# Two transformer layers with gated cross-attention: ScalarE places the negated maxima and stores the bounds

## The chip, the cores and the metric

The kernel runs on one core of a Trainium2 chip. The core has a matrix engine (TensorE, PE), a vector engine (VectorE, DVE), a scalar engine (ScalarE, ACT), GpSimd (POOL), a sync engine (SP) whose instructions start transfers, and 16 DMA engines. Each engine works through its own list of instructions in order, and they wait for each other by semaphores. The metric is the device time of one execution in microseconds.

## What is computed

The input is `x` (8 batches x 256 rows x 256) and a context (8 x 256 x 192). Four steps follow each other, each added to `x` behind a normalisation and with a gate: cross-attention, a mixture of experts, cross-attention again (with scores clipped to +-10000), and a second mixture of experts. The two attentions matter here:

```python
q = (x @ q_w + q_b).reshape(B, N, H, hd).transpose(0, 2, 1, 3)      # 16 heads of 16
attn = jnp.einsum('bhnd,bhmd->bhnm', q * scale, k)
attn = jnp.clip(attn, -CLAMP, CLAMP)                                # layer 1 only
attn = jax.nn.softmax(attn, axis=-1)
out = jnp.einsum('bhnm,bhmd->bhnd', attn, v)
```

A softmax over the keys needs the largest score of each query first, so that the exponential does not overflow.

## The kernel before

**Units and pairs.** A unit is one batch of one attention: units 0 to 7 are layer 0, units 8 to 15 layer 1. In a unit the 16 heads are taken as 8 pairs: heads 0 to 7 are side 0, heads 8 to 15 side 1, and pair p is head p of either side. A function `base(u)` gives the time slot in which unit u begins; a unit takes 8 slots, one pair in each. Layer 0's experts (`gate_up`, `down0`: L849, L859) fill the slots from about 105 us to 530 us, so TensorE has products to do beside both attentions. The second experts run alone at the end.

**The scores are computed twice.** `scores_by_query(u, p)` (L752) makes a pair's scores with queries on the partitions; VectorE takes the row maxima (`maxima`, L1368). Ten slots later `scores_by_key(u, p)` (L773) makes them again with keys on the partitions, which is the form that the product with the values needs, and ScalarE takes the exponential (`exponentials`, L1162). There the maximum must be subtracted along the free dimension, and TensorE does it: queries and keys are stacked in tiles `stack_q` and `stack_k`, side 0 on partitions 0 to 63 and side 1 on 64 to 127. Of each side 48 rows are the high and low parts of the 16 features; rows 48 and 49 of `stack_q` hold the negated maximum of each query in two parts, and the same rows of `stack_k` hold ones.

**How the maxima get there.** When a unit's 8 pairs are through (slot `base(u)` + 7), `shifts(u)` on VectorE (L1379 to L1382) writes three rows of 32 numbers per query tile: the high part, the low part, and for layer 1 the lower bound -max - 10000. In slot `base(u)` + 8 TensorE turns them (`shift_turn`, L759) and ScalarE copies them to `shiftT` (L1151; in layer 1 L1150 writes the exponential of the bounds first). Then the sync queue's `place_shift(u)` waits for `shiftT_ready` and issues four transfers (L566), one for each side and part, each into one partition of `stack_q`, and in layer 1 a fifth, L569, which stores the bounds to DRAM. `scores_by_key(u, 0)`, two slots later, waits for the four (`shift_in`). In layer 1 the sync queue's `load_lower` (L577) waits for the stored bounds (`lower_out`) and loads a pair's, spread over all partitions; VectorE's `clip` (L1393) uses them.

**What stands around it in the queues.** The order of every engine's work is written out by `make_plan`: an entry at `2g` or `2g + 1` belongs to slot g. `shift_turn` of unit u is put in front of `qprod` of unit u+2, at the same entry. So ScalarE's list has, in slot `base(u)` + 8: the exponential of a pair of the unit before, `shift_turn(u)`, and `qprod(u + 2)`, which copies the high part of the queries (L1074). VectorE subtracts it to get the low part (L1359), and both are stored to DRAM by the sync queue (`store_queries`, L529 and L532), which stands behind `place_shift(u)` in that queue. Units 14 and 15 have no `qprod` there. Three PSUM banks serve all products but the scores and the values in turn; a product may take its bank only when the one three uses before has been read, and the bank of `qprod` counts as read when L1359 is done. ScalarE issues few transfers of its own: five small ones at the start, and the queries of unit 0 (L1079, L1082), each behind a wait for the instruction that wrote them.

Of the kernel before, what the change touches and what calls it, by code (L numbers as in the profile page):

```python
# [12 lines left out]
F32 = mybir.dt.float32  # L13
F32R = mybir.dt.float32r
# [3 lines left out]
ALU = mybir.AluOpType  # L18
# [7 lines left out]
H, HD = 16, 16  # L26
TT = S // P
# [15 lines left out]
CLAMP = 10000.0  # L43
# [5 lines left out]
FULL = PARTS * HD  # L49
HALF = 64  # L50
PAIRS = H // 2
# [5 lines left out]
SETS = 3  # L57
# [36 lines left out]
def layer_of(u):  # L94
    return u // NB


def batch_of(u):
    return u % NB


def base(u):

    return LEAD + PAIRS * u
# [143 lines left out]
def build(nc, a, out):  # L248
    es = ExitStack()
    first = ExitStack()  # L250
    sem = Semaphores(*[es.enter_context(nc.semaphore(name)) for name in SEMAPHORES])
# [5 lines left out]
    def sba(name, shape, dt=F32):  # L257
        return first.enter_context(nc.sbuf_tensor(name, shape, dt))

    qk_dram = [nc.dram_tensor(f"qk_{l}", (NB, 4, D, S), F32).ap() for l in range(2)]  # L260
    lower_dram = nc.dram_tensor("lower", (NB, H * TT, P), F32).ap()
# [38 lines left out]
    stack_q = [sba(f"stack_q{i}", [P, PAIRS, S], F32R) for i in range(SETS)]  # L300
# [18 lines left out]
    rowmax = [sba(f"rowmax{i}", [P, 2, PAIRS, TT]) for i in range(2)]  # L319
    shift = sba("shift", [P, 3, H * TT])  # L320
    shiftT = sba("shiftT", [3 * H * TT, P])
# [113 lines left out]
    def _(sp):  # L435
# [121 lines left out]
                    o = HALF * side + blk * HD  # L557
                    sp.dma_start(stack_q[i][o:o + HD, :, :].bitcast(F32), src[side]).then_inc(q_in[i], 16)

        def place_shift(u):  # L560
            l, b = layer_of(u), batch_of(u)
            sp.wait_ge(sem.shiftT_ready, u + 1)
            for side in range(2):
                for part in range(2):
                    row, src = HALF * side + FULL + part, (2 * part + side) * PAIRS * TT
                    sp.dma_start(stack_q[u % SETS][row:row + 1, :, :].bitcast(F32).rearrange("o a (t q) -> o (a t) q", t=TT),  # L566
                                 shiftT[src:src + PAIRS * TT, :]).then_inc(sem.shift_in, 16)
            if l:
                sp.dma_start(lower_dram[b], shiftT[2 * H * TT:3 * H * TT, :]).then_inc(sem.lower_out, 16)  # L569

        def load_lower(u, p):
            b = batch_of(u)
            j = PAIRS * b + p
            if j >= 3:
                sp.wait_ge(sem.clip_done, j - 2)
            sp.wait_ge(sem.lower_out, 16 * (b + 1))
            sp.dma_start(lower[j % 3][:, :, :], lower_dram[b].rearrange("(h a t) q -> a h (t q)", h=2, t=TT)[p]  # L577
                         .partition_broadcast(P)).then_inc(lower_in[j % 3], 16)

        def store_alternative(_):  # L580
            sp.wait_ge(sem.zalt_ready, 1)
            sp.dma_start(zalt_dram[:, :], zalt).then_inc(sem.zalt_out, 16)

        def load_alternative(_):
            sp.wait_ge(sem.zalt_out, 16)
            sp.wait_ge(sem.y_done, N0 * NB)
            sp.dma_start(alt_rows.rearrange("p b d -> p (b d)"),
                         zalt_dram.rearrange("b d -> (b d)").partition_broadcast(P)).then_inc(sem.zalt_in, 16)
# [30 lines left out]
        def first_weights(_):  # L619
            sp.wait_ge(sem.counted, NB)  # L620
            sp.dma_start(b1[:, :], a["L1_ffn_b1"]).then_inc(sem.biases_in, 16)
            sp.wait_ge(sem.block_ready, 1)
            for i in range(2):
                load_w1(i)

        def store_rows(b):
# [5 lines left out]
        load_x(0)  # L632
        load_ctx(0)
        stages = {"load": load, "ctx": context, "kprod": store_keys, "qprod": store_queries, "stack_keys": stack_keys, "stack_queries": stack_queries,
                  "shift_turn": place_shift, "mean_project": store_alternative, "project": store_z, "reload": reload, "load_expert": load_expert, "load_alternative": load_alternative,
                  "weights1": store_rows, "bias1": store_x, "tables": first_weights}
        for g in range(SLOTS_IN_ALL):
            for stage, n in PLAN[2 * g - 3] + PLAN[2 * g - 2]:
# [2 lines left out]
            u, p = divmod(g + 1 - base(0) - LAG, PAIRS)  # L641
# [12 lines left out]
    def _(pe):  # L654
# [6 lines left out]
        def stay_busy(n, bank):  # L661

            for _ in range(n):
                pe.matmul(bank[:, 0:P], ident[:, :], ident[:, :], start=True, stop=True)
# [97 lines left out]
        def scores_by_key(u, p):  # L762
            i, sq, sk = PAIRS * u + p, stack_q[u % SETS], stack_k[u % SETS]
            if p == 0:
                pe.wait_ge(sem.shift_in, 64 * (u + 1))
            if i:
                pe.wait_ge(sem.exp_done, i)
            if i < PAIRS:
                stay_busy(2, by_key[:, 0, :])
            for kt in range(2):  # L770
                for side in range(2):
                    rows = slice(HALF * side, HALF * side + HALF)
                    mm = pe.matmul(by_key[:, side, kt * S:kt * S + S], sk[rows, p, kt * P:kt * P + P], sq[rows, p, :],  # L773
                                   start=True, stop=True)
            mm.then_inc(sem.qk2_done, 1)
# [46 lines left out]
        def gate_turn(_):  # L822
            bank = open_bank("gate_turn", 0)
            pe.wait_ge(sem.gates_in, 64)
            for k in range(KC):
                tr = pe.transpose(bank[:, k * E0:k * E0 + E0], gate_rows[:, k * P:k * P + P], ident[0:E0, 0:E0])
            tr.then_inc(sem.gate_turned, 1)
# [35 lines left out]
        def spread_nan(_):  # L863
            bank = open_bank("spread_nan", 0)
            pe.wait_ge(sem.flag_ready, 1)
            pe.matmul(bank[:, 0:1], ones[:, :], flag[:, 1:2], start=True, stop=True).then_inc(sem.flag_mm, 1)

        def mean_v(_):
            bank = open_bank("mean_v", 0)
            pe.wait_ge(sem.ctxT_ready, NB)  # L870
            for k in range(2):
                mm = pe.matmul(bank[0:NB, 0:D], ctx_sum[:, k, :], wkv[1][0:CROWS, k, D:2 * D], start=k == 0, stop=k == 1)
            mm.then_inc(sem.mean_mm, 1)
# [67 lines left out]
        for g in range(SLOTS_IN_ALL):  # L941
            v, q = divmod(g - base(0), PAIRS)
            if 0 <= v < UNITS:
                scores_by_query(v, q)
            u, p = divmod(g - base(0) - LAG, PAIRS)
# [7 lines left out]
            u, p = divmod(g - base(0) - LAG - 3, PAIRS)  # L953
# [90 lines left out]
    def _(ac):  # L1044
# [96 lines left out]

        def shift_turn(u):
            if u:
                ac.wait_ge(sem.shift_in, 64 * u)
            if u > NB:
                ac.wait_ge(sem.lower_out, 16 * (u - NB))
            bank, bounds = banks[BANK_OF["shift_turn", u][0]], slice(2 * H * TT, 3 * H * TT)
            ac.wait_ge(sem.shift_turned, u + 1)
            if layer_of(u):
                ac.activation(shiftT[bounds, :], bank[bounds, 0:P], ACT.Exp)  # L1150
            ac.activation(shiftT[0:2 * H * TT, :], bank[0:2 * H * TT, 0:P], ACT.Copy).then_inc(sem.shiftT_ready, 1)  # L1151

        def gates(_):
            ac.wait_ge(sem.gates_in, 32)
            ac.activation(tg[:, :], g_raw[:, :], ACT.Tanh).then_inc(sem.gates_ready, 1)
# [60 lines left out]
        for g in range(SLOTS_IN_ALL):  # L1216
# [3 lines left out]
            u, p = divmod(g - base(0) - LAG, PAIRS)  # L1220
# [81 lines left out]
    def _(dv):  # L1302
# [66 lines left out]
                             AX, ALU.max).then_inc(sem.max_done, 1)  # L1369

        def shifts(u):
            flat = rowmax[u % 2][:, :, :, :].rearrange("p h a t -> p (h a t)")
            dv.wait_ge(sem.max_done, PAIRS * (u + 1))
            if layer_of(u):
                dv.tensor_scalar(flat, flat, CLAMP, -CLAMP, ALU.min, ALU.max).then_inc(sem.shift_chain, 1)
                dv.wait_ge(sem.shift_chain, u + 1 + batch_of(u))
            if u:
                dv.wait_ge(sem.shift_turned, u)
            dv.tensor_scalar(shift[:, 0, :].bitcast(F32R), flat, -1.0, None, ALU.mult).then_inc(sem.shift_chain, 1)  # L1379
            dv.tensor_scalar(shift[:, 2, :], flat, -1.0, -CLAMP, ALU.mult, ALU.add).then_inc(sem.shift_ready, 1)  # L1380
            dv.wait_ge(sem.shift_chain, u + 1 + (batch_of(u) + 1 if layer_of(u) else 0))
            dv.scalar_tensor_tensor(shift[:, 1, :].bitcast(F32R), flat, -1.0, shift[:, 0, :], ALU.mult,  # L1382
                                    ALU.subtract).then_inc(sem.shift_ready, 1)

        def clip(u, p):
# [374 lines left out]
        for g in range(SLOTS_IN_ALL):  # L1760
# [7 lines left out]
            v, q = divmod(g - base(0), PAIRS)  # L1768
# [7 lines left out]
            u, p = divmod(g - base(0) - LAG - 1, PAIRS)  # L1776
# [216 lines left out]
```

## Time and profile before

| what | value |
|---|---|
| median of 3 runs | 982.74 us (978.57 to 985.58) |
| the profiled execution | 982.38 us |
| its span | 980.6 us |
| granted clock of TensorE, mean | 0.951 |
| busy: TensorE, VectorE, ScalarE, GpSimd | 92%, 75%, 48%, 26% |
| sync queue, wait for ScalarE's copy L1151 | 68.3 us in 14 waits |
| placing transfers L566 | 64 of 8 KB, issue median 0.589 us |

The span is the time from the first to the last instruction of the profiled execution. A granted clock of 1.00 is full speed, 0.50 the lower level. An engine's busy share is an average over stages with different limits, so the rows below are taken from single stretches. SPq and ACTq are the parts of the sync engine and of ScalarE that issue transfers; issuing is not counted as busy.

### The profile page before, as it was taken

How to read it: one execution, taken by the hardware profiler on the slowest of the kernel's cores; microseconds unless marked ns; L12 is line 12 of the kernel's file. 1: busy time of each engine (PE TensorE's matmuls, PEld its weight loads, DVE VectorE, ACT ScalarE, POOL GpSimd, SP SyncE). 2: the span in 40 equal slices, each digit the busy share in tenths (PEclk: the TensorE clock that was granted, in tenths of full speed). 3: DMA queues.
4: the chain of work that ended last, by engine and by line, in shares of the span. 5: the costliest groups of instructions: out<-in, count | busy, mean ns of one | idle time of the engine just before them, and what ended most of it. 6: DMA issues, size and time to landing. Idle time of an engine off the chain costs nothing.

```text
span 980.6 us, 18579 instructions
## 1 busy us (share of the span) xinstructions
PE 905.1 (92%) x6641; PEld 746.2 (76%) x6641; DVE 740.2 (75%) x1516; ACT 471.6 (48%) x835; POOL 252.5 (26%) x385
## 2 busy tenths in 40 slices
PE   7998999999999998999988877899899999999995
PEld 6766677777767766777756554667799999999995
DVE  4555767677676767798887898978868788887783
ACT  2245544444534343344433444443356666666773
POOL 7511011020210000010101113323136566543331
PEclk9999999999999999999999977769799999999998
DMA  6977866146152346474655873342387777777772
GB/s 167 181 147 153 185 184 118 48 80 110 41 78 56 63 83 106 76 154 98 130 115 101 186 210 106 96 125 63 121 266 221 215 217 220 221 220 217 231 249 44
DMA packets 128523, 139.69 MB, mean 142 GB/s; under 512 B 12336, under 2 KB 121160, under 8 KB 128304
## 3 DMA queue, kind: packets, MB, share of 16 engines
q1 hardware_dynamic: 119296, 127.59, 52.5%
q0 software_dynamic: 7488, 10.39, 5.0%
q8 instruction: 53, 0.87, 0.4%
q10 hardware_dynamic: 1648, 0.53, 0.3%
q14 instruction: 38, 0.31, 0.1%
HBM read 108.50 MB, written 29.44 MB: 141 GB/s over the span
## 4 chain that ended last, share of the span: by engine, by line
PE 65%; DVE 18%; issue 5%; DMA 4%; ACT 3%; POOL 2%; SPq 1%; POOLq 0%; DVEq 0%; ACTq 0%
PE bank L1024 11%; PE bank L849 9%; PE by_query L1008 7%; PE by_key L1008 7%; PE bank L859 5%; DVE rowmax L1368 4%; PE value_bank L791 4%; PE by_query L752 3%; DVE probs L1393 3%; PE bank L694 3%; PE bank L738 2%; PE bank L818 2%; PE by_key L773 2%; PE bank L703 2%; DMA lower<-lower 2%
## 5 line engine op out<-in xcount | busy, mean ns | idle before, releaser
L1162 ACT ACTIVATE probs<-by_key 128x1024 f32<-128x1024 f32 x128 | 130.7, 1021 | 99.3 <-PE by_key L773 98.8
L1368 DVE TENSOR_REDUCE rowmax<-by_query 128x4 f32<-128x1024 f32 x128 | 155.6, 1215 | 27.5 <-PE by_query L752 27.5
L1903 POOL TENSOR_SCALAR rstd<-moments 128x2 f32<-128x2 f32 x32 | 10.5, 327 | 490.3 <-DVE moments L1324 490.2
L1970 POOL DMA_INDIRECT out_x<-x,token_i x39 | 68.7, 1763 | 124.3 <-ACT x L1271 94.2
L752 PE MATMUL by_query<-stack_k,stack_q 48*128 48x256 f32 x512 | 67.3, 342 | 25.3 <-DVE rowmax L1368 23.7
L1024 PE MATMUL bank<-w_hi,h_hi 128*128 128x256 f32 x312 | 88.3, 283 | 0.0
L1024 PE MATMUL bank<-w_lo,h_hi 128*128 128x256 f32 x312 | 88.3, 283 | 0.0
L1024 PE MATMUL bank<-w_hi,h_lo 128*128 128x256 f32 x312 | 88.3, 283 | 0.0
L752 PEld LDWEIGHTS by_query<-stack_k,stack_q 48*128 48x128 f32 x512 | 40.3, 194 | 63.0 <-DVE rowmax L1368 35.3
L791 PE MATMUL value_bank<-probs,values 128*32 128x256 f32 x1024 | 76.9, 423 | 10.5 <-DVE probs L1393 10.3
L859 PE MATMUL bank<-w_down,hidden 128*128 128x256 f32 x288 | 79.8, 400 | 3.8 <-DVE summed L1431 1.8
L849 PE MATMUL bank<-xnT,w_gate 128*128 128x256 f32 x288 | 79.6, 400 | 3.1 <-DVE lo L1359 2.4
L1393 DVE SCALAR_TENSOR_TENSOR probs<-probs,lower 128x1024 f32<-128x1024 f32 x64 | 78.0, 1220 | 5.9 <-DMA lower<-lower 5.9
L1195 ACT ACTIVATE act_gate<-bank 128x256 f32<-128x256 f32 x72 | 27.6, 383 | 106.4 <-PE bank L849 106.4
L849 PE MATMUL bank<-xnT,w_up 128*128 128x256 f32 x288 | 77.0, 391 | 0.0
L1526 DVE SCALAR_TENSOR_TENSOR x<-bank,expert_cols,x 128x256 f32<-128x256 f32 x144 | 62.4, 475 | 14.3 <-PE bank L859 14.3
L1957 POOL DMA_INDIRECT xs_in<-rows,token_i x39 | 61.7, 1583 | 32.0 <-DVE token_i L1788 20.4
L849 PEld LDWEIGHTS bank<-xnT,w_gate 128*128 128x128 f32 x288 | 52.9, 194 | 15.6 <-DVE lo L1359 3.4
L1792 DVE TENSOR_TENSOR w_lo<-w,w_hi 128x2048 fp32r<-128x2048 f32 x23 | 52.7, 2292 | 14.7 <-ACT w_hi L1234 14.4
L859 PEld LDWEIGHTS bank<-w_down,hidden 128*128 128x128 f32 x288 | 50.4, 192 | 17.0 <-issue 3.7
L849 PEld LDWEIGHTS bank<-xnT,w_up 128*128 128x128 f32 x288 | 56.8, 197 | 8.4
L1508 DVE SCALAR_TENSOR_TENSOR act_t<-act_gate,bank 128x256 f32<-128x256 f32 x72 | 30.1, 419 | 43.6 <-ACT act_gate L1195 42.8
(267 smaller groups left out, 2257.8 us busy)
## 6 DMA issues: line engine op xcount, KB each, us to landing
w<-in_L_ffn_W SPq DMA_DIRECT2D x46, 1024.0 KB, 7.3
lower<-lower SPq DMA_DIRECT2D x64, 256.0 KB, 5.5
stack_k<-qk SPq DMA_DIRECT2D x96, 128.0 KB, 4.9
stack_q<-qk SPq DMA_DIRECT2D x96, 128.0 KB, 6.7
qk<-hi SPq DMA_DIRECT2D x31, 256.0 KB, 2.4
qk<-lo SPq DMA_DIRECT2D x31, 256.0 KB, 2.7
rows<-w_gate SPq DMA_DIRECT2D x8, 264.0 KB, 4.7
x<-in_x SPq DMA_DIRECT2D x8, 256.0 KB, 6.4
```

The costliest lines, as they stand in the source:

```text
L752: mm = pe.matmul(by_query[:, side, t * S:t * S + S], sq[rows, p, t * P:t * P + P], sk[rows, p, :], start=True, stop=True)
L791: mm = pe.matmul(value_bank[32 * c:32 * c + 32, o:o + S], values[u % 2][:, kt, 4 * j + c, :], probs[(i + c // 2) % 4][:, kt, c % 2, :], st ...
L849: mm = pe.matmul(bank[:, half * S:half * S + S], w[:, k, e, :], turned_of(("ffn0", b))[:, k, :], start=k == 0, stop=k == 1)
L859: mm = pe.matmul(bank[:, t * D:t * D + D], hidden0[i % 6][:, t * P:t * P + P], w_down0[:, e, :], start=True, stop=True)
L1008: mm = pe.matmul(up_bank[pair][:, half * SLOTS:half * SLOTS + SLOTS], wt[:, k, j * P:j * P + P], xt[:, k, :], start=n == 0, stop=n == len( ...
L1024: mm = pe.matmul(bank[:, t * D:t * D + D], ht[:, j, t * P:t * P + P], wt[:, j, :], start=j == 0 and t == 0 and n == 0, stop=j == JH - 1 an ...
L1162: ac.activation(probs[i % 4][:, :, :, :].rearrange("p k h s -> p h k s"), by_key[:, :, :].rearrange("p h (k s) -> p h k s", k=2), ACT.Exp) ...
L1368: dv.tensor_reduce(rowmax[u % 2][:, :, p, :], by_query[:, :, :].rearrange("p h (t s) -> p h t s", t=TT), AX, ALU.max).then_inc(sem.max_don ...
L1393: dv.scalar_tensor_tensor(prob, prob, 1.0, bound, ALU.min, ALU.max).then_inc(sem.clip_done, 1)
L1526: op = dv.scalar_tensor_tensor(xt, bank[:, t * D:t * D + D], expert_cols[b % 2][:, t, e:e + 1], xt, ALU.mult, ALU.add)
L1957: po.indirect_dma_start(xs_in[i % 4][:, t, :], None, xn1_dram[:, :], bass.IndirectOffsetOnAxis(ap=token_i[:, tiles_to(i) + t:tiles_to(i) + ...
L1970: po.indirect_dma_start(out[:, :], bass.IndirectOffsetOnAxis(ap=token_i[:, n:n + 1].bitcast(U32), axis=0), ysb[i % 3][:, t, :], None, comp ...
```

## The change

`place_shift` leaves the sync queue. ScalarE's `shift_turn` does its work: behind the copy it waits for the copy's own semaphore, issues one transfer for each side, and in layer 1 the store of the bounds. For one transfer to carry both parts of a side, VectorE's `shifts` writes them in another order: side 0 high, side 0 low, side 1 high, side 1 low. The waits for `shift_in` count 32 a unit in place of 64.

```diff
-        def place_shift(u):
-            l, b = layer_of(u), batch_of(u)
-            sp.wait_ge(sem.shiftT_ready, u + 1)
-            for side in range(2):
-                for part in range(2):
-                    row, src = HALF * side + FULL + part, (2 * part + side) * PAIRS * TT
-                    sp.dma_start(stack_q[u % SETS][row:row + 1, :, :].bitcast(F32).rearrange("o a (t q) -> o (a t) q", t=TT),
-                                 shiftT[src:src + PAIRS * TT, :]).then_inc(sem.shift_in, 16)
-            if l:
-                sp.dma_start(lower_dram[b], shiftT[2 * H * TT:3 * H * TT, :]).then_inc(sem.lower_out, 16)
...
-                  "shift_turn": place_shift, "mean_project": store_alternative, "project": store_z, "reload": reload, "load_expert": load_expert, "load_alternative": load_alternative,
+                  "mean_project": store_alternative, "project": store_z, "reload": reload, "load_expert": load_expert, "load_alternative": load_alternative,
...
-                pe.wait_ge(sem.shift_in, 64 * (u + 1))
+                pe.wait_ge(sem.shift_in, 32 * (u + 1))
...
-                ac.wait_ge(sem.shift_in, 64 * u)
+                ac.wait_ge(sem.shift_in, 32 * u)
...
             ac.activation(shiftT[0:2 * H * TT, :], bank[0:2 * H * TT, 0:P], ACT.Copy).then_inc(sem.shiftT_ready, 1)
+            ac.wait_ge(sem.shiftT_ready, u + 1)
+            for side in range(2):
+                row, src = HALF * side + FULL, side * H * TT
+                ac.dma_start(stack_q[u % SETS][row:row + 2, :, :].bitcast(F32).rearrange("o a (t q) -> o (a t) q", t=TT),
+                             shiftT[src:src + H * TT, :]).then_inc(sem.shift_in, 16)
+            if layer_of(u):
+                ac.dma_start(lower_dram[batch_of(u)], shiftT[2 * H * TT:3 * H * TT, :]).then_inc(sem.lower_out, 16)
...
-            flat = rowmax[u % 2][:, :, :, :].rearrange("p h a t -> p (h a t)")
+            flat = rowmax[u % 2][:, :, :, :].rearrange("p h a t -> p h (a t)")
+            by_side = shift[:, 0:2, :].rearrange("p j (o r) -> p (j o) r", o=2)
+            hi, lo = by_side[:, 0:4:2, :], by_side[:, 1:4:2, :]
...
-            dv.tensor_scalar(shift[:, 0, :].bitcast(F32R), flat, -1.0, None, ALU.mult).then_inc(sem.shift_chain, 1)
-            dv.tensor_scalar(shift[:, 2, :], flat, -1.0, -CLAMP, ALU.mult, ALU.add).then_inc(sem.shift_ready, 1)
+            dv.tensor_scalar(hi.bitcast(F32R), flat, -1.0, None, ALU.mult).then_inc(sem.shift_chain, 1)
+            dv.tensor_scalar(shift[:, 2, :].rearrange("p (h r) -> p h r", h=2), flat, -1.0, -CLAMP, ALU.mult, ALU.add).then_inc(sem.shift_ready, 1)
...
-            dv.scalar_tensor_tensor(shift[:, 1, :].bitcast(F32R), flat, -1.0, shift[:, 0, :], ALU.mult,
+            dv.scalar_tensor_tensor(lo.bitcast(F32R), flat, -1.0, hi, ALU.mult,
```

## Rows read from the trace of the kernel before

**Rows 1.** Windows: stretch, length, busy us of each engine, clock, DMA share, GB/s
```profile
110.00:150.00 40.00, 38.85 (x266) 29.24 (x266) 29.12 (x74) 16.88 (x30) 5.47 (x17) 1.00 0.74 169
550.00:590.00 40.00, 32.37 (x237) 22.09 (x233) 32.92 (x53) 19.03 (x32) 7.90 (x18) 0.79 0.89 220
```

**Rows 2.** Waits of the sync queue: us in total, times, longest
```profile
SPq L566 <- ACT shiftT L1151: 68.3, 14, 19.4
...
SPq L576 <- DMA lower<-shiftT: 5.9, 6, 1.4
```

**Rows 3.** Waits of all engines
```profile
DVE probs L1393 <- DMA lower<-lower: 5.9, 3, 3.2
```

**Rows 4.** The tile shiftT: duration min/median/max, then the transfers' landing
```profile
L566 SPq DMA_DIRECT2D stack_q<-shiftT x64: 502/589/1487, 53.4 to 639.6; - x64
...
L569 SPq DMA_DIRECT2D lower<-shiftT x8: 578/578/1610, 356.6 to 640.3; - x8
...
DMA to landing us min/median/max: 1.7/2.2/3.8
```

**Rows 5.** Timeline behind unit 4's copy: start us, duration us
```profile
181.50 3.32 SPq L566 DMA_DIRECT2D stack_q<-shiftT  x4
```

**Rows 6.** The chain that ended last, 14 to 18 us: start, us
```profile
15.98 0.85 ACT hi L1074 x2
```

**Rows 7.** Line L1079, a transfer that ScalarE issues
```profile
L1079 ACTq DMA_DIRECT2D qk<-hi x1: 413/413/413, 16.8 to 16.8; - x1
```

**Rows 8.** Timeline at unit 3
```profile
138.62 0.26 ACT L1151 ACTIVATE shiftT<-bank 64x128 f32<-64x128 f32 x1
...
139.67 0.84 ACT L1074 ACTIVATE hi<-bank,qkb 128x256 fp32r<-128x256 f32 x2 [0.79 <-PE bank L738]
...
141.54 0.70 PE L849 MATMUL bank<-xnT,w_gate 128*128 128x256 f32 x2 [0.67 <-DVE lo L1359]
```

**Rows 9.** Timeline at unit 7
```profile
307.90 0.26 ACT L1151 ACTIVATE shiftT<-bank 64x128 f32<-64x128 f32 x1
308.06 0.46 ACT L1074 ACTIVATE hi<-bank,qkb 128x256 fp32r<-128x256 f32 x1
...
310.11 0.66 PE L801 MATMUL bank<-ident,weighted 128*128 128x128 f32 x4 [0.77 <-DVE lo L1359]
```

**Rows 10.** Timeline at unit 12
```profile
534.23 0.27 ACT L1151 ACTIVATE shiftT<-bank 64x128 f32<-64x128 f32 x1
...
534.87 0.47 ACT L1074 ACTIVATE hi<-bank,qkb 128x256 fp32r<-128x256 f32 x1 [0.37 <-PE bank L738]
...
536.96 1.13 PE L849 MATMUL bank<-xnT,w_gate 128*128 128x256 f32 x4 [0.89 <-DVE lo L1359]
```

**Rows 11.** Timeline at units 9 and 10
```profile
403.17 0.88 DVE L1359 SCALAR_TENSOR_TENSOR lo<-bank,qkb,hi 128x256 fp32r<-128x256 f32 x2 [1.34 <-ACT hi L1074]
...
404.10 1.13 PE L859 MATMUL bank<-w_down,hidden 128*128 128x256 f32 x4
...
444.51 0.20 ACT L1074 ACTIVATION_READ_ACCUMULATOR hi<-bank,qkb 128x1 f32 x1
...
445.37 0.87 DVE L1359 SCALAR_TENSOR_TENSOR lo<-bank,qkb,hi 128x256 fp32r<-128x256 f32 x2
```

**Rows 12.** Timeline at unit 1: the copy, and the first pair's scores by key
```profile
77.66 0.26 ACT L1151 ACTIVATE shiftT<-bank 64x128 f32<-64x128 f32 x1
...
82.67 0.40 PE L773 MATMUL by_key<-stack_q,stack_k 64*128 64x256 f32 x4
```

**Rows 13.** DMA queues of the page: packets, MB, share of 16 engines' span
```profile
q1 hardware_dynamic: 119296, 127.59, 52.5%
```

**Rows 14.** Windows, as rows 1, before and in a stretch at the lower clock
```profile
388.00:392.00 4.00, 2.29 (x8) 1.59 (x8) 2.22 (x3) 0.93 (x2) 0.00 (x0) 0.78 0.34 53
392.00:396.00 4.00, 4.00 (x16) 2.96 (x15) 2.60 (x7) 1.02 (x1) 0.00 (x0) 0.50 0.62 94
```

## The prediction

> **What bounds the kernel now.** I read the engines' windows first. In attention layer 0 TensorE is busy 38.85 of 40 us at a clock of 1.00; late in layer 1 it is 32.37 of 40 at 0.79, VectorE 32.92, ScalarE 19.03 [rows 1]. So in the first layer any new idle time of TensorE is lost, and in the second TensorE and VectorE take turns. The experts behind them don't touch the change. Next I read who waits for the moved transfers. The sync queue waits 68.3 us for ScalarE's copy, in 14 waits, and 5.9 us for `lower_out` [rows 2]: it stands ready when the copy ends and is no backlog that the change could remove. TensorE has no wait on `stack_q<-shiftT` in any answer; VectorE waits 5.9 us, three times, for a load of `lower` [rows 3]. Last I read the timeline behind each copy (L1151), since that is where ScalarE would stop.
>
> **What is moved.** The sync queue issues 64 placing transfers at a median of 0.589 us and 8 stores of the bounds at 0.578 us [rows 4]: 64 x 0.589 + 8 x 0.578 = 42 us of its time. They become 32 + 8 on ScalarE's queue. ScalarE's price for this shape is not in the trace. The upper end is 0.83, from the group of four that took 3.32 us at unit 4 [rows 5]. The new wait of ScalarE for its own copy costs nothing: where it waits so already, L1074 ends at 15.98 + 0.85 = 16.83 [rows 6] and the guarded transfer L1079 starts at 16.8; that issue took 0.413 us, of another shape, which is the lower end [rows 7]. I take 0.589: the same source tile and the same rows of 512 B. So ScalarE is blocked for 0.03 + 2 x 0.59 = 1.21 us behind the copy in layer 0, and for 0.03 + 2 x 0.59 + 0.58 = 1.79 us in layer 1.
>
> **What is queued behind it.** For units 0 to 13 the next ScalarE instruction is L1074, the high part of the queries of unit u+2. VectorE's L1359 needs it, and TensorE needs L1359 before it takes the same bank again, three uses on. The delay is the block less the gap that now lies between the copy's end and L1074.
> - Unit 3, the pattern of layer 0: the copy ends at 138.88, L1074 starts at 139.67, and TensorE's L849 waited 0.67 us for L1359 [rows 8]. Gap 0.79, delay 1.21 - 0.79 = 0.42, all of it felt. Unit 1 the same. Units 4 to 6 have this gap too, but L1359 ends a little before it is needed; with the middle slack of rows 11, 0.35, each feels 0.07.
> - Units 2 and 7 have no gap. At unit 7 the copy starts at 307.90 and L1074 at 308.06, 0.10 us before the copy's end; L801 waited 0.77 us for L1359 [rows 9]. Delay 0.10 + 1.21 = 1.31 at each.
> - Unit 0 has a gap longer than the block and feels nothing.
> - Unit 12, the pattern of layer 1: the copy ends at 534.50, L1074 starts at 534.87, L849 waited 0.89 us for L1359 [rows 10]. Gap 0.37, delay 1.79 - 0.37 = 1.42, felt whole. Units 8 and 13 the same: 4.26 for the three.
> - Units 9 to 11 have slack. At unit 9 L1359 ends at 403.17 + 0.88 = 404.05 and L859 starts at 404.10: 0.05. At unit 10 L1074's last part ends at 444.51 + 0.20 = 444.71 and L1359 starts at 445.37: 0.66 [rows 11]. Unit 11 I put between them, 0.35. Felt: 1.37 + 0.76 + 1.07 = 3.20.
> - Units 14 and 15 have no L1074 behind the copy; I cost them at nothing. The cover is a TensorE wait for row maxima and VectorE's routing work; without it they would cost 1.8 us each.
>
> Layer 0: 2 x 0.42 + 3 x 0.07 + 2 x 1.31 = 3.7 us, kept whole, since TensorE has 3% of idle there. Layer 1: 4.26 + 3.20 = 7.5 us, of which I keep two thirds, 5.0, since a delay of one engine can run into a wait that the other had anyway. Sum **8.7 us**. At 0.41 an issue the same working gives 2.0 + 4.2 us, about 3 if half is recovered. At 0.83 it gives 7 + 12 = 19 us, nothing recovered.
>
> **What comes back.** Now the fourth placing transfer starts 0.03 + 3 x 0.60 = 1.8 us behind the copy and lands 2.2 us on [rows 4], at 4.0. Then the second starts at 0.6 and, if it lands as today's do, is there at 2.8. That is worth nothing where `scores_by_key(u, 0)` comes later, and the shortest distance is at unit 1: the copy ends at 77.92, L773 for its first pair starts at 82.67, 4.75 us on [rows 12]. The bounds' store goes 1.2 us behind the copy, not 2.4, and opens `lower_out` 1.2 us earlier; of the three waits in rows 3 the one behind such a load is the shortest, and I give it 0.2 us. The 42 us of the sync queue are on no path: what stands behind them is the store of L1074's result. VectorE's three small instructions write four runs of 16 for one of 32; I cost that at nothing, their length being start-up, and 0.05 us each if it is not, under TensorE's current product. Gain: 0.2 us.
>
> The profiled execution took 982.4 us (a span of 980.6 and 1.8 around it), 0.4 under the median of 982.7. 982.4 + 8.7 - 0.2 = **991 us**.
>
> **A rule against the change.** Each old transfer writes one partition in 16 rows of 512 B; each new one writes two partitions. No row of the trace shows one of the second form. The Trainium skill (DMA: Bandwidth & Descriptors, "Why a DMA increments its semaphore by 16 and not by 1") says that a transfer from these queues runs on the largest number of engines up to 16 that divides the slowest dimension of both sides. By that rule, which no run here shows yet, a new placement would have 2 engines where an old one had 16; what it would do here is rival 1.
>
> **Rivals.**
> 1. *Placement late.* A mean packet of the sync queue took 0.525 x 16 x 980.6 / 119296 = 0.069 us [rows 13]. If the 16 rows of a side follow each other on one engine they take 1.1 us, and 2.2 where packets of another queue alternate, on top of today's worst landing of 3.8 us [rows 4]: 0.6 + 3.8 + 2.2 = 6.6 us behind the copy. Against 4.75 us [rows 12] TensorE waits up to 1.9 us at unit 1; I take 1.2 us at each of five units, 6 us, beside the forecast's 8.5: 997. For it: a DMA share of 0.74 to 0.89 [rows 1]. Against: half of today's landings take 2.2 us or less. It decides from a landing of 4.1 us on. Chance 0.12.
> 2. *TensorE's clock (the slower side).* The idle stretches that grow are those before the readers of L1359: 0.67, 0.77 and 0.89 us [rows 8 to 10] become up to 2.3. In 388 to 392 us TensorE was busy for 2.29 of 4 us, and in the next 4 us it ran at 0.50, the 1.2 GHz level [rows 14]; such a row costs 2 us. Four more are 8 us: 999. Against: unit 3's wait lies in a window at 1.00 [rows 1]. It decides at units 2, 7, 8 and 12, once their wait passes what the clock bears. Chance 0.13.
> 3. *Covered.* The delays fall into other waits, or ScalarE issues in 0.3 us: 982 to 985. For it: ScalarE is under half busy [rows 1]. Against: TensorE waits for L1359 in three of the patterns above. Chance 0.22.
> 4. *The bounds decide (faster).* If each unit of layer 1 went at the pace of `lower_out`, 8 x 1.2 = 9.8 us would go: 972.6. For it: the sync queue waited for `lower_out` 6 times [rows 2]. Against: VectorE waited 5.9 us in all for any bound [rows 3]. Chance 0.10.
>
> **The numbers.** The forecast, 991 with a range of its own from 986 to 997, has 0.43. About 1%, 9.8 us, is what a measurement can tell here, so the borders are 972.9 and 992.6. Faster: most of rival 4, 0.08. Slower: two fifths of the forecast's case and nearly all of rivals 1 and 2, 0.17 + 0.23 = 0.40. Within 1%: the rest, 0.52. The range holds both ends of the unknown price, most of rival 4, and rivals 1 and 2: 974 to 1002.
>
> **What the profile after would show.** ScalarE's transfers of 0.59 us right behind L1151; L1074 starting 1.2 us (layer 0) or 1.8 us (layer 1) behind the copy's end in place of 0.79 and 0.37; TensorE's waits for L1359 longer by 0.4 to 1.4 us, above all at units 2, 7, 8 and 12; the stretch before 350 us longer by 4 us, that of layer 1 by 5. Rival 1 shows as a wait for `stack_q<-shiftT` and landings over 4 us, rival 2 as new rows at 0.50, rival 4 as units of layer 1 shorter by 1 us each. I am wrong if ScalarE's transfers take 0.3 us or less, if L1074's delay does not reach TensorE, or if the clock between 550 and 660 us changes for reasons of its own, which could outweigh the sum either way.

## The result, and the profile after

The changed kernel takes **1005.0 us** (median of 4 runs, 995.75 to 1008.97), the kernel before beside it 982.4. The ratio is 1.0218, with a 95% interval from 1.0134 to 1.0303. A second measurement with more runs gave 1.0238 [1.0201, 1.0275]. I had forecast 991 with a range up to 1002: the sign and the place were right, and the size was 2.7 times too small (22.6 us against 8.5). The profiled execution took 995.75 us, the shortest of its runs, and the profile therefore shows only a part of the loss; two more profiles follow below. From here on every median, ratio and clock is of the undisturbed executions alone; a few others ran at a lower granted clock (one of run 1: 1126.8 us at 0.735) and are left out.

The two windows of [rows 1], now of the kernel after (stretch, length, busy us of each engine, clock, DMA share, GB/s):

```profile
110.00:150.00 40.00, 38.20 (x266) 28.79 (x267) 26.84 (x71) 17.36 (x32) 3.36 (x9) 1.00 0.77 170
550.00:590.00 40.00, 31.37 (x231) 21.03 (x229) 32.12 (x51) 16.84 (x28) 2.69 (x8) 0.85 0.73 173
```

TensorE is busy 0.65 us less in the first and 1.0 us less in the second. Fixed windows mislead here: both kernels do different parts of the work in them, and the clock of the second even looks better than before. I therefore cut the later comparisons at the copies, which mark the same work in both.

The tile shiftT after, as in [rows 4] (duration min/median/max in ns, then the landing), and the issues of the same execution with their size and median landing:

```profile
L1144 ACTq DMA_DIRECT2D stack_q<-shiftT x32: 621/622/1256, 53.5 to 653.2; - x32
...
L1147 ACTq DMA_DIRECT2D lower<-shiftT x8: 422/422/423, 360.6 to 653.9; - x8
...
DMA to landing us min/median/max: 1.8/3.2/4.7
```

```profile
stack_q<-shiftT ACTq DMA_DIRECT2D x32, 16.0 KB
lower<-shiftT ACTq DMA_DIRECT2D x8, 16.0 KB, 3.2
```

A placement takes ScalarE 0.62 us (I took 0.589), the store 0.42 us (0.578). The landing needs care: the profile gives none for the 32 merged placements, so 3.2 us is the median of the 8 stores alone (2.2 us before). The placements' own landing can be read from the updates of their semaphore `shift_in` in the trace. The last update for a unit comes 3.0 us behind the copy in the median of the 16 units, where it came 4.05 us behind before; at unit 1 it is 2.9 against 3.7 us. So the maxima are in place a microsecond earlier than before. The store lands 4.6 us behind the copy (median of 8), against 5.1 before.

The timeline at unit 3, to be held against [rows 8] (start, duration):

```profile
142.61 0.26 ACT L1140 ACTIVATE shiftT<-bank 64x128 f32<-64x128 f32 x1
142.90 1.27 ACTq L1144 DMA_DIRECT2D stack_q<-shiftT  x2
...
144.27 0.84 ACT L1063 ACTIVATE hi<-bank,qkb 128x256 fp32r<-128x256 f32 x2 [1.41 <-PE bank L727]
...
146.16 1.13 PE L838 MATMUL bank<-xnT,w_gate 128*128 128x256 f32 x4 [1.28 <-DVE lo L1355]
```

And at unit 12, against [rows 10]:

```profile
545.33 0.27 ACT L1140 ACTIVATE shiftT<-bank 64x128 f32<-64x128 f32 x1
...
545.63 1.30 ACTq L1144 DMA_DIRECT2D stack_q<-shiftT  x2
...
546.97 0.42 ACTq L1147 DMA_DIRECT2D lower<-shiftT  x1
547.49 0.47 ACT L1063 ACTIVATE hi<-bank,qkb 128x256 fp32r<-128x256 f32 x1 [1.89 <-issue]
...
549.58 1.34 PE L838 MATMUL bank<-xnT,w_gate 128*128 128x256 f32 x4 [2.40 <-DVE lo L1355]
```

This is the predicted chain, link by link. The transfer starts 0.03 us behind the copy's end (142.87), so ScalarE's wait for its own copy costs nothing. The high part of the queries (L1063, before L1074) starts 1.40 us behind the copy in layer 0 and 1.89 us in layer 1, where it was 0.79 and 0.37. TensorE waits 1.28 us for the low part where it waited 0.67, and 2.40 where it waited 0.89. Note the releaser at unit 3: the row names TensorE's product L727, which had been done for 0.7 us; what really held L1063 is the transfer above it, and at unit 12 the row says "issue" for the same thing.

The waits (us in total, times, longest), as [rows 2, 3] gave them before:

```profile
DVE lo L1355 <- ACT hi L1063: 38.0, 15, 3.9
...
ACT hi L1063 <- issue: 14.4, 8, 2.2
...
DVE probs L1391 <- DMA lower<-lower: 7.2, 3, 4.3
```

and the same view of TensorE alone:

```profile
PE bank L838 <- DVE lo L1355: 6.0, 3, 2.4
...
PE bank L848 <- DVE lo L1355: 3.9, 4, 1.5
PE bank L790 <- DVE lo L1355: 3.8, 3, 2.3
...
PE bank L717 <- DVE lo L1355: 2.2, 1, 2.2
```

TensorE's waits for the low part are 6.0 + 3.9 + 3.8 + 2.2 = 15.9 us. In the kernel before the same four lines, not shown among the rows ahead of the prediction, are:

```profile
PE bank L849 <- DVE lo L1359: 2.4, 3, 0.9
...
PE bank L801 <- DVE lo L1359: 0.8, 1, 0.8
PE bank L728 <- DVE lo L1359: 0.7, 1, 0.7
...
PE bank L859 <- DVE lo L1359: 0.5, 1, 0.5
```

That is 4.4 us, so these waits grew by **11.5 us**. No wait of TensorE for `stack_q<-shiftT` has appeared: rival 1 is false. VectorE's wait for the bounds is 7.2 us in place of 5.9, so rival 4 has nothing to stand on.

The sync queue waits longer for the bounds' store than before, and it now waits for ScalarE at what used to be its next piece of work:

```profile
SPq L529 <- ACT hi L1063: 109.5, 15, 21.5
...
SPq L565 <- DMA lower<-shiftT: 13.6, 5, 5.6
```

It has only become idler (5.9 us before for the second row, [rows 2]); the relief of 42 us of its time bought nothing.

### The profile page after: what moved, and what is told of

Read it like the earlier page. It is cut to its first block, busy times and chain, and to the rows that moved or that the text cites. A ratio compares the mean times of both kernels' runs of the same rounds, so it can differ in the third digit from the quotient of the medians.

```text
span 994.0 us, 18547 instructions
## 1 busy us (share of the span) xinstructions
PE 902.8 (91%) x6641; PEld 744.4 (75%) x6641; DVE 739.7 (74%) x1516; ACT 470.6 (47%) x835; POOL 253.9 (26%) x385
## 4 chain that ended last, share of the span: by engine, by line
PE 61%; DVE 18%; issue 6%; ACT 4%; DMA 4%; POOL 2%; ACTq 2%; SPq 2%; DVEq 0%; POOLq 0%
PE bank L1013 11%; PE bank L838 9%; PE by_query L997 7%; PE by_key L997 7%; PE bank L848 5%; DVE rowmax L1364 4%; PE value_bank L780 4%; PE by_query L741 3%; PE bank L683 3%; DVE probs L1391 3%; PE bank L807 2%; ACTq L1144 2%; PE by_key L762 2%; PE by_query L653 2%; PE bank L692 2%
## 5 line engine op out<-in xcount | busy, mean ns | idle before, releaser
L1506 DVE SCALAR_TENSOR_TENSOR act_t<-act_gate,bank 128x256 f32<-128x256 f32 x72 | 30.0, 417 | 42.9 <-ACT act_gate L1191 42.1
```

## The experiments

There were eleven further runs, three of them of the two kernels themselves (1, 10, 11). **Theory A**: what costs is the time for which ScalarE is held ahead of the queries' high part. **Theory B**: the merged, two-partition form of the transfer, or its place on another queue, costs by landing later. **Theory C**: what A's waits don't explain is TensorE's clock.

**1. The changed kernel again** (no edit).

> The changed kernel once more, for its level and for what its slower runs consist of. Its profiled run took 995.75 us at a mean clock of 0.954, three others 1002 to 1009 at 0.942 to 0.949. Theory A (ScalarE's block, 1.4 us in layer 0 and 1.9 us in layer 1, delays the queries' high part and with it TensorE) gives about +12 us against the kernel before in the waits for the low part, in every run. Theory C (the longer idle stretches make the clock fall more often) gives the rest, some 5 to 12 us, and it must show as a lower mean clock in the longer runs. Both together: ratio 1.015 to 1.03. If the time does not go with the clock, theory C falls.

1002.7 us, ratio 1.0238 [1.0201, 1.0275]. Its waits for the low part are the same to 0.1 us. The loss is firm. As theory C asked, the longer executions have the lower clock in the main: 0.952 at 1000.3 us, 0.942 at 1006.7.

**2. The transfers behind the high part.** ScalarE still issues both transfers and the store, but only after L1063 of unit u+2.

```
 def qprod(u):                      # ScalarE
     ...
     op.then_inc(sem.q_hi, 1)
+    if u >= 2:
+        place_shift(u - 2)
 def shift_turn(u):
     ...
-    (the wait, two transfers and the store)
+    if u + 2 >= UNITS:
+        place_shift(u)
```

> The same transfers on ScalarE, but issued behind the high part of the queries of unit u+2 in place of ahead of it (units 14 and 15 as in the change). Theory A: the delay of the high part goes, the placement comes 1 us later than in the change, which nobody waits for; 982 to 987 us, ratio to the kernel before 1.000 to 1.005. Theory B (the new form of the transfers, two partitions at a time, lands late, and TensorE or the loads of the bounds wait for it): it stays near the change, 995 to 1005, since the form and the queue are the change's.

985.1 us, ratio 1.0050 [1.0021, 1.0079]. All of TensorE's waits for the low part are back at 4.4 us. With ScalarE's queue and the merged form kept, four fifths of the loss are gone: A holds, and the order on ScalarE is what does it. The placement itself starts later still here; TensorE waited for it once, 0.2 us. What remains (2 to 8 us by the interval) I have not divided further, and its cause is open. VectorE waited 9.7 us for the bounds in this run's profile, where it was 5.9, but it waited 9.9 us in run 4 as well, whose transfers are those of the kernel before.

**3. The change on the sync queue.** VectorE's new order and two merged transfers a unit, issued where the four stood.

```
 sp.wait_ge(sem.shiftT_ready, u + 1)
 for side in range(2):
-    for part in range(2):
-        row, src = HALF * side + FULL + part, (2 * part + side) * PAIRS * TT
-        sp.dma_start(stack_q[u % SETS][row:row + 1, ...
+    row, src = HALF * side + FULL, side * H * TT
+    sp.dma_start(stack_q[u % SETS][row:row + 2, ...
```

> VectorE's new order and the two transfers per unit, but issued by the sync queue as before; ScalarE issues none. Theory A: as the kernel before, 980 to 985 us, ratio 0.997 to 1.003. Theory B: most of the loss stays, 992 us or more, with a landing of 3 us or more where it was 2.2. The landing itself should be near 3.2 us in either case, as in the change.

981.5 us, ratio 1.0020 [0.9993, 1.0048]: no change that can be told. The tile's rows of this run:

```profile
L564 SPq DMA_DIRECT2D stack_q<-shiftT x32: 610/617/792, 56.3 to 639.5; - x32
...
L567 SPq DMA_DIRECT2D lower<-shiftT x8: 407/408/417, 355.0 to 640.2; - x8
```

The landing that the profile gives, again of the 8 stores alone, was 3.0 us here and 2.1 us in run 9, where the store stood behind four transfers on ScalarE's queue. But run 8, in which nothing is merged and the store is issued first, has 3.7 us. The store's later landing therefore goes with its earlier issue; that the merged form delays it isn't shown. The placements landed 3.1 us behind the copy here (median of the 16 units), as in the changed kernel, and no time was lost that can be told: the form is no cause. VectorE's scattered writes cost nothing that can be told either. Of theory B this leaves the place on ScalarE's queue, which run 2 keeps.

**4 and 5. The holding alone.** The kernel before, its transfers untouched, with idle copies of 256 columns on ScalarE behind the copy; first 3 (layer 0) and 4 (layer 1), then 5 and 7.

```
 ac.activation(shiftT[0:2 * H * TT, :], bank[0:2 * H * TT, 0:P], ACT.Copy).then_inc(sem.shiftT_ready, 1)
+(a wait for the idle copies of the unit before, long done)
+for i in range(7 if layer_of(u) else 5):       # run 4: 4 and 3
+    op = ac.activation(idle_out[:, i, :], zero_row[:, 0:256], ACT.Copy)
+(the last one counts up a semaphore for that wait)
```

> The kernel before, with its four transfers on the sync queue, and ScalarE doing useless copies (128 x 256) behind its own copy to shiftT: three in layer 0 (about 1.3 us), four in layer 1 (about 1.7 us), in the place where the change issues its transfers. Theory A: it costs about what the change costs, 993 to 1005 us, ratio 1.012 to 1.023. Theory B: nothing of it, 983 us, since no transfer differs from the kernel before.

989.5 us, ratio 1.0070 [1.0036, 1.0103]. The copies turned out shorter than I had reckoned: ScalarE was held for 0.82 and 1.12 us only, and the waits grew by 4.6 us (to 9.0).

> The kernel before, with idle copies of 256 columns behind the copy of the negated maxima: 5 in layer 0 and 7 in layer 1, at 0.27 to 0.28 us each by the run of 3 and 4, so that ScalarE is held for 1.4 and 1.9 us, as long as the changed kernel's transfers hold it. The transfers stay on the sync queue as they were. Theory A (only the time in which ScalarE is held counts): TensorE's waits for the low part of the queries grow by 11 to 12 us, as in the changed kernel, and the time goes up by as much as there, ratio 1.018 to 1.028. Theory B (half of the loss comes from the transfers being on ScalarE's queue: their landing, what they do to other transfers): the waits grow alike, but the ratio stays at 1.009 to 1.014. If the first sees the loss only with a lower clock in the timed runs, the clocks of the runs beside it fall as the changed kernel's did, from 0.955 to 0.948.

999.0 us, ratio **1.0178 [1.0145, 1.0211]**. L1076 started 1.43 and 2.05 us behind the copy, and the waits grew by 12.4 us:

```profile
PE bank L851 <- DVE lo L1369: 6.6, 3, 2.5
...
PE bank L861 <- DVE lo L1369: 4.2, 4, 1.7
PE bank L803 <- DVE lo L1369: 3.7, 3, 2.3
...
PE bank L730 <- DVE lo L1369: 2.3, 1, 2.3
```

Without one DMA moved, three quarters of the loss are there (17.5 of 23 us): theory A, just under the range that I had given it, and the interval leaves out theory B's 1.009 to 1.014. The quarter that is missing, about 6 us, is as large as what stayed in run 2 (5 us). Both would fit a smaller cost of having the transfers on ScalarE, but the intervals of run 5 and of the changed kernel just overlap and no run isolates it. And the time grew by more than the waits, which no theory with waits alone explains.

**6 and 7. One layer each.** In the changed kernel ScalarE issues in one layer and the sync queue, with the same merged transfers, in the other.

```
+if layer_of(u) == 0:               # run 7: == 1
     ac.wait_ge(sem.shiftT_ready, u + 1)
     (the two transfers and the store by ScalarE)
```

> The changed kernel, but ScalarE places only in layer 0 (two transfers a unit); in layer 1 the sync queue issues the two transfers and the store. Forecast's own sizes: layer 0 alone costs 3.7 us, ratio 1.004. By the waits of TensorE that the trace of the changed kernel shows for units 2 to 7 (4.5 us more than before) and the factor of 1.6 to 2 seen between waits and time: 7 to 9 us, ratio 1.007 to 1.009.

991.1 us, ratio 1.0114 [1.0076, 1.0152]: above the 7 to 9 us that I had expected, though its interval reaches them.

> The changed kernel, but ScalarE places and stores only in layer 1; in layer 0 the sync queue issues the two merged transfers. The forecast (a third of layer 1's delays is recovered): 5.0 us, ratio 1.005. Nothing recovered: 7 to 7.5 us, 1.0075. Waits lengthened further by the clock: 12 to 15 us, 1.012 to 1.015, with a lower mean clock than the run of layer 0 alone, since layer 1 is where the clock is below 1.

992.1 us, ratio 1.0101 [1.0063, 1.0139]. Together 2.15%, against 2.38% for the whole: the layers add up. Layer 0, for which I had 3.7 us, costs 11; layer 1, for which I had kept 5.0 of 7.5 us, costs 10. Its interval (6 to 14 us) leaves room for 7.5 and for 12, and none for 5.0.

**8. The bounds' store first** (kernel before).

```
 sp.wait_ge(sem.shiftT_ready, u + 1)
+if l:
+    sp.dma_start(lower_dram[b], ...).then_inc(sem.lower_out, 16)
 (the four placing transfers)
-if l:
-    sp.dma_start(lower_dram[b], ...).then_inc(sem.lower_out, 16)
```

> The kernel before, with one edit: in layer 1 the sync queue issues the store of the bounds ahead of the four placing transfers instead of behind them, so that it goes 2.4 us earlier (four issues of 0.59) and the placings 0.58 us later. If the bounds decide the pace of layer 1 (the fourth rival, 1.2 us in each of 8 units): up to 9.8 us less, ratio 0.990. If only VectorE's three waits for a load of the bounds count (5.9 us in all): 0 to 4 us less, 0.996 to 1.0. If the placings were near being late: slower. I expect no change within 0.3%.

980.4 us, ratio 0.9999 [0.9971, 1.0027]. The store was issued 2.4 us earlier and landed 1.4 us earlier (3.7 us behind the copy in place of 5.1), more than the change gives it, and nothing came of it. Rival 4 is excluded by a run and not only by the wait rows; that the placings went 0.33 us later (the store's issue took that here) cost nothing.

**9. Twice the dose.** The four unmerged transfers and the store, all by ScalarE behind the copy.

```
 ac.activation(shiftT[0:2 * H * TT, :], ...).then_inc(sem.shiftT_ready, 1)
+ac.wait_ge(sem.shiftT_ready, u + 1)
+(the four placing transfers and the store of the kernel before, by ScalarE)
```

> The kernel before with its four placing transfers and the store unmerged, but issued by ScalarE right behind the copy. Theory A (the time in which ScalarE is held counts): at 0.62 us each ScalarE is held for 2.6 us in layer 0 and 3.1 us in layer 1 instead of 1.4 and 1.9, that is 1.2 us more at each of 12 units whose low part is waited for, 14 us beyond the changed kernel, so 37 us above the kernel before, ratio 1.035 to 1.045. If merging had shortened only the landing and ScalarE took 0.41 us for the one-partition form, as it did for its other guarded transfer: held for 1.8 and 2.3 us, ratio 1.027 to 1.032. If later waits take the delay up (a covering work of other engines), the ratio stays near 1.024.

1029.8 us, ratio **1.0509 [1.0469, 1.0549]**, above all that I had expected. L1063 starts 2.6 us behind the copy in layer 0 and 3.2 us in layer 1, and the waits are:

```profile
PE bank L838 <- DVE lo L1356: 11.0, 3, 4.7
PE bank L848 <- DVE lo L1356: 9.6, 4, 2.8
PE bank L790 <- DVE lo L1356: 7.2, 3, 3.5
...
PE bank L717 <- DVE lo L1356: 3.4, 1, 3.4
```

31.2 us, 26.8 more than before; the time grew by 50. The waits are near what theory A foresaw (11.5 + 14 us); the time is not.

**10 and 11. More profiles** of the kernel before and the one after.

> The kernel before once more, for a second profile: how much of the stretch from unit 3's copy to unit 15's (498.9 us in the first profile, 496.1 in the run with the bounds' store first, which has the same waits) changes from one execution to another. I expect 496 to 500, with the stretch before unit 3's copy ending between 138 and 143 us.

980.3 us. Unit 3's copy ended at 140.0 us, as expected. The stretch from there to unit 15's copy took 494.9 us, below the 496 to 500 that I had given: one kernel's stretch differs by 4 us between two executions.

> The changed kernel once more, for a third profile. If what is missing between the waits and the time is the clock at the start of layer 0 and behind unit 12, then the stretch from unit 3's copy to unit 15's is 509 to 511 us again, and the copy of unit 3 ends between 142.8 and 147 us; the time is 995 to 1005 us, by that start.

1001.2 us. Of its forecasts the sum from unit 3's copy to unit 15's (507.6 us) came a little short, and unit 3's copy ended at 148.12 us, later than I had given. Now the same work can be laid side by side: one window from the end of unit 1's copy to the end of unit 15's (columns as in the first fence). First the kernel before, in two executions:

```profile
77.92:637.79 559.87, 513.89 (x3512) 380.46 (x3510) 432.96 (x986) 247.44 (x452) 73.13 (x211) 0.95 0.53 111
```

```profile
79.02:634.91 555.89, 509.70 (x3512) 379.67 (x3510) 432.54 (x986) 247.15 (x453) 74.22 (x211) 0.95 0.52 112
```

Then the kernel after, in three (the profile after, run 1, run 11):

```profile
78.20:652.53 574.33, 515.29 (x3512) 381.78 (x3510) 432.52 (x987) 246.65 (x452) 74.46 (x211) 0.94 0.53 108
```

```profile
79.84:657.10 577.26, 517.75 (x3512) 382.51 (x3510) 432.46 (x987) 246.79 (x452) 74.43 (x211) 0.94 0.51 108
```

```profile
81.76:655.75 573.99, 516.35 (x3512) 382.95 (x3510) 432.35 (x986) 246.60 (x453) 73.03 (x211) 0.94 0.53 108
```

And the four transfers by ScalarE:

```profile
83.03:683.79 600.76, 529.23 (x3512) 390.57 (x3510) 432.70 (x986) 246.07 (x452) 73.08 (x211) 0.92 0.48 103
```

All have 3512 matmuls there, and VectorE and ScalarE are busy for the same time within 1.4 us. TensorE is not: its busy time is 511.8 us before (mean of two), 516.5 after (of three), 529.2 with four. The window is 557.9, 575.2 and 600.8 us. So after, 17.3 us more = 11.5 of waits + 4.7 of *the same matmuls running longer* + 1.1 else. With four transfers, 42.9 more = 26.8 + 17.4, less 1.3. The second term is the clock, since the work is the same, and in places one can see where it comes from. Unit 7 in windows of 4 us, before:

```profile
308.00:312.00 4.00, 2.90 (x13) 2.10 (x14) 2.68 (x8) 1.07 (x6) 0.00 (x0) 1.00 0.10 29
312.00:316.00 4.00, 4.00 (x38) 2.58 (x36) 2.73 (x6) 2.01 (x3) 0.00 (x0) 1.00 0.45 147
```

and after, where TensorE's wait of 2.28 us ends at 314.76:

```profile
312.00:316.00 4.00, 1.72 (x8) 1.21 (x7) 2.13 (x6) 1.02 (x4) 0.00 (x0) 0.86 0.31 106
316.00:320.00 4.00, 4.00 (x18) 2.94 (x18) 1.30 (x5) 0.75 (x2) 0.00 (x0) 0.72 0.12 40
```

In these 8 us, around and behind the longer wait, the mean clock is 0.79: 0.14 x 4 + 0.28 x 4 = 1.7 us of full clock were not granted, on top of a wait that grew by 1.5. From unit 7's copy to unit 8's it takes 47.9 us in place of 45.1: 2.8, close to 1.5 + 1.7. The other profiles bear this out. Wherever unit 7's wait had grown, in run 4 only from 0.8 to 1.7 us, this stretch takes 47.7 to 48.8 us (runs 1, 4, 5, 6, 9 and 11); where it is untouched, 45.1 in every one (runs 2, 3, 7, 8 and 10). In run 11 a low stretch lies behind unit 1 too (start of the row, length, busy, ..., clock):

```profile
88.00:92.00 4.00, 3.48 (x27) 1.85 (x26) 1.83 (x2) 2.57 (x7) 0.00 (x0) 0.54 0.39 101
92.00:96.00 4.00, 4.00 (x17) 2.77 (x16) 0.17 (x1) 1.01 (x3) 0.00 (x0) 0.61 1.13 151
```

It costs 3.1 us: unit 1 to unit 2 takes 28.5 us there, and 25.4 in the first profile after, at a clock of 1.00; in both profiles of the kernel before it is 24.8. But unit 1 has no wait for the low part, so what brought this one on is not shown.

**What the timed runs say of the clock.** Each run has its span and its mean granted clock c. A span times (1 - c) is the full clock that was not granted in it, whether TensorE had work there or not. Taking the means of the timed runs, and TensorE's waits for the low part from each kernel's one profile (all in us; clock and waits are growth over the kernel before, whose clock was 0.957 to 0.958; "measured" is the ratio's excess times 980.6):

| kernel | mean clock | clock | waits | sum | measured |
|---|---|---|---|---|---|
| after, again (1) | 0.948 | 11 | 11.5 | 23 | 23 |
| behind the high part (2) | 0.956 | 2 | 0 | 2 | 5 |
| two by the sync queue (3) | 0.955 | 2 | 0 | 2 | 2 |
| held 0.8/1.1 us (4) | 0.955 | 4 | 4.6 | 8 | 7 |
| held 1.4/2.0 us (5) | 0.952 | 7 | 12.4 | 19 | 17 |
| layer 0 alone (6) | 0.952 | 6 | 4.7 | 11 | 11 |
| layer 1 alone (7) | 0.950 | 8 | 7.2 | 15 | 10 |
| bounds first (8) | 0.958 | -1 | 0 | -1 | 0 |
| four by ScalarE (9) | 0.934 | 26 | 26.8 | 53 | 50 |

The two terms give the time within 3 us in eight kernels of nine; layer 1 alone is 5 off. But this sum takes a microsecond of clock not granted for a microsecond of time, and that is too much. The kernel before took 974.5 us at 0.970 and 988.3 at 0.946: 24 us more of clock not granted in the second, and 14 us more time. Over its 58 executions beside these runs one microsecond goes with 0.52 of time. At that weight the clock accounts for 6 of the changed kernel's 23 us and, with the waits, 5 are left over. In the profiled windows it was 4.7 of 17.3. So the clock is a quarter of the loss to, at most, half; the agreement of the table is no proof of the half. That a held ScalarE lowers the clock is shown by run 5 (0.952), with no DMA touched. The rule by which one wait costs clock and the next doesn't is not settled by these runs.

No version beats the kernel before: the best are the bounds first (0.9999) and the two merged transfers on the sync queue (1.0020).

## Why the prediction fell short, step by step

- **The chain** (copy, high part, low part, TensorE's bank) was right in each link, and so were most of the units: 2, 7, 8, 9 and 12 grew most (by 1.5 us each), units 4 to 6 least (0.2 to 0.45).
- **ScalarE's block** was sized 1.21 and 1.79 us and measured 1.40 and 1.88. The issue price was nearly right (0.62 for 0.589); the rest is 0.1 us between the last transfer's end and the next instruction (142.90 + 1.27 = 144.17 against 144.27).
- **The raw delays** came to 3.7 + 7.5 us. Measured by TensorE's waits they are 4.7 + 6.8 = 11.5. That the sums are so close is partly luck: units 1 and 13, to which I gave 0.42 and 1.42 by likeness to their neighbours, show no such wait before or after, and all the other units from 2 to 12 felt more than I had given them, by 0.09 to 0.38 us each.
- **The step that failed** is the last one, from delays to time. I let the 11.2 us of delays cost 8.7, and they came with a loss of 22 to 23. It has two parts. The smaller, 2.5 us, is in layer 1: "of which I keep two thirds, 5.0, since a delay of one engine can run into a wait that the other had anyway". Nothing was recovered, neither in the waits (6.8 us) nor in the time (run 7: 10 us). TensorE and VectorE do take turns there; that this wait stands at the head of a chain on which VectorE hangs, and so shifts both, is my reading and not tested.
- **The clock was made a rival in place of a term.** This is the larger part of the failed step: the sum put at nothing what it costs. I gave four more rows of 4 us at 0.50, 8 us in all, a chance of 0.13 as a case of its own, 999 in place of 991. It isn't an alternative to the delays but what they bring with them. With the recovery not taken off (11.2 in place of 8.7) and those 8 us on top the sum would have been 982.4 + 11.2 + 8 - 0.2 = 1001, against 1003 to 1005 measured. How much of the 11 us beyond the waits is the clock (5 to 11) and how much the 5 us that remained in run 2 is open. I had argued against it from unit 3, whose wait of 0.67 us lies in a window at 1.00; that says what 0.67 us bears, and nothing of 2.3 us.
- **Rival 1** (placement late) failed because the merged placements are not slow. In layer 0 a unit's last one lands 2.2 to 2.4 us behind its issue, against 1.9 for the last of the four before, and since it is issued 1.1 us earlier it lands earlier behind the copy. My 6.6 us for the worst was too high: it is 5.5 us, at unit 13, and nobody waited for it. The Trainium skill (DMA: Bandwidth & Descriptors, "Why a DMA increments its semaphore by 16 and not by 1") ties the number of engines to the slowest dimension, which gives 2 engines for a merged placement and 16 for an old one. It says that each engine adds one to the semaphore when it is done and that the issuing side adds the rest at once. The trace agrees: 96 updates of `shift_in` for the 32 merged transfers, three for each, and 1024 for the 64 old ones, sixteen for each.
- **Rival 3** (covered) fails by the 11.5 us by which the waits grew; **rival 4** by run 8. The gain of 0.2 us can't be seen: VectorE's wait for the bounds is 7.2, 7.6 and 6.1 us in the three profiles after and 5.9 and 6.1 in the two before. The store is issued 1.2 us earlier and lands only 0.5 earlier.
- **Costed at nothing**, and rightly: VectorE's scattered writes and the merged form (run 3), the wait of ScalarE for its own copy.

The same page of the Trainium skill (section "Issuing engines are not separate DMA queues") says that issuing from another engine only saves the sequencer's issue time, which it calls usually small relative to the DMA. The first half agrees with run 9: the store landed 2.1 us behind its issue on ScalarE's queue and 2.2 on the sync queue before. The second half is true of the numbers too, 0.61 us of issue against a landing of 2.1 for the same placement in run 9, but it is the wrong comparison here: on a computing engine the issue stands ahead of that engine's next instruction.

## What to carry to other kernels

Moving a transfer from an idle queue to a computing engine costs its issue time (0.4 to 0.6 us here) wherever that engine's next instruction is in a chain that the bottleneck waits for; look at what is queued right behind it, and if it must go there, issue it behind that instruction (run 2 gave back four fifths). A queue that waits 68 us for its input is not a queue that needs relief. And when a change lengthens TensorE's waits, add the clock to the waits and don't weigh it against them: here each us of added wait went with 1.4 to 2.4 us of time, and 1.9 at the largest dose. And before a median landing is compared, look which transfers it is of.

## What the runs showed of the hardware

- The same store took the sync queue 0.578 us behind four placements, 0.408 behind two and 0.33 when it stood first; ScalarE's queue took 0.594 behind four (run 9) and 0.422 behind two (medians). The price of an issue went with what was issued just ahead, and hardly with the engine. The store's landing went the other way: 3.7 us when it stood first, 3.0 to 3.2 behind two, 2.1 to 2.2 behind four.
- A low stretch comes and goes between executions of one kernel. From unit 4's copy to unit 5's the kernel before took 42.1 us at a clock of 0.96 in one profile and 40.5 at 1.00 in the other; the kernel after takes 41.1 at 1.00, 0.6 more than the latter, with a wait that grew by 0.45.
- The granted clock tells the executions of one kernel apart as well: the kernel before took from 974.5 us at 0.970 to 988.3 at 0.946.
